# One-hot compares with a pointer scalar, and a second feature gathered in unit 0 (recommendation tower, one core)

## The reference, cut to what matters

```python
e = jnp.stack([tbl_0[ids[:, 0]], ..., tbl_26[ids[:, 26]]], axis=1)    # 2048 x 27 x 128
dot_products = jnp.einsum('bnd,bmd->bnm', e, e)
r, c = np.tril_indices(27, k=-1)
z = dot_products[:, c, r].reshape(2048, -1)
h = jnp.concatenate([z, dense_ctx], axis=1)                           # 2048 x 367
h = jnp.maximum(h @ W_top1 + b_top1, 0.0)                             # 512
h = jnp.maximum(h @ W_top2 + b_top2, 0.0)                             # 256
y = h @ W_top3
```

## Time and profile before

| what | us |
|---|---|
| median of three runs | 354.51 (354.46 to 360.79) |
| the profiled execution | 354.21 |
| its span, first to last instruction | 352.1 |
| around the span (354.21 - 352.1) | 2.1 |

### The profile page before, as it was taken

The page is one execution under the profiler, slowest core; times in us unless marked ns, Lnnn a source line. Parts: engine busy times, 40 slices in busy tenths (PEclk is TensorE's granted clock), DMA queues, the critical chain, the costliest instruction groups (busy, mean ns, idle before and its releaser), DMA issues.

```text
span 352.1 us, 12745 instructions
## 1 busy us (share of the span) xinstructions
PE 330.7 (94%) x5664; PEld 278.9 (79%) x5664; DVE 250.9 (71%) x335; ACT 148.8 (42%) x304; POOL 244.4 (69%) x265
## 2 busy tenths in 40 slices
PE   1897879999999999999999999999999999999986
PEld 0686768888888888888888888888888888887775
DVE  3899999989839696587929698487938786420322
ACT  2256543443534254433644245442545246535321
POOL 5777776777777777777777777777777777777100
PEclk9999999999999999999999999999999999999999
DMA  7997574443433433243332433243342332222000
GB/s 219 323 270 244 128 217 104 99 116 92 122 85 90 108 85 103 55 119 85 90 94 77 107 99 80 77 114 85 89 98 59 83 95 71 57 57 59 20 4 3
DMA packets 21928, 36.81 MB, mean 105 GB/s; under 512 B 7907, under 2 KB 12003, under 8 KB 21874
## 3 DMA queue, kind: packets, MB, share of 16 engines
q0 software_dynamic: 8256, 16.92, 19.7%
q1 hardware_dynamic: 13474, 18.55, 18.0%
q10 hardware_dynamic: 144, 0.52, 0.4%
HBM read 35.97 MB, written 0.01 MB: 102 GB/s over the span
## 4 chain that ended last, share of the span: by engine, by line
PE 87%; DVE 8%; issue 2%; DMA 1%; ACT 1%; SPq 0%; DVEq 0%
PE e_banks L560 42%; PE g_banks L594 13%; PE w_banks L624 10%; PE e_banks L572 9%; PE w_banks L655 8%; DVE one_hot L781 5%; DVE table_lo L762 3%; PE w_banks L644 2%; DMA ids_wide<-in_ids 1%; PE w_banks L613 1%; PE w_banks L666 0%; DVE g_banks L768 0%; DVE a L829 0%; ACT et L410 0%; DVE zt L795 0%
## 5 line engine op out<-in xcount | busy, mean ns | idle before, releaser
L528 POOL DMA_INDIRECT rows<-in_tbl,idx x258 | 243.6, 944 | 82.1 <-issue 77.4
L781 DVE TENSOR_TENSOR one_hot<-ids_wide,row_no 128x1024 fp32r<-128x1024 int32 x160 | 183.9, 1216 | 25.4 <-PE e_banks L560 21.4
L560 PE MATMUL e_banks<-one_hot,table_hi 128*128 128x512 f32 (+1 forms) x448 | 151.8, 356 | 5.3 <-issue 5.1
L560 PE MATMUL e_banks<-one_hot,table_lo 128*128 128x512 f32 (+1 forms) x448 | 147.2, 345 | 0.0
L560 PEld LDWEIGHTS e_banks<-one_hot,table_hi 128*128 128x128 f32 x448 | 85.5, 191 | 18.3 <-issue 7.6
L560 PEld LDWEIGHTS e_banks<-one_hot,table_lo 128*128 128x128 f32 x448 | 85.6, 191 | 9.2
L410 ACT ACTIVATE et<-e_banks 128x256 f32<-128x256 f32 x56 | 38.9, 694 | 84.7 <-PE e_banks L560 84.5
L402 ACT ACTIVATE et<-e_banks 128x512 f32<-128x512 f32 (+1 forms) x66 | 44.0, 668 | 51.5 <-PE e_banks L572 50.3
L795 DVE STREAM_TRANSPOSE zt<-g_banks 128x352 f32<-128x352 f32 (+1 forms) x32 | 17.8, 595 | 53.2 <-PE g_banks L594 53.2
L594 PEld LDWEIGHTS g_banks<-et 128*26 128x26 f32 x4096 | 42.0, 103 | 16.9 <-issue 13.2
L594 PE MATMUL g_banks<-et 128*26 128x26 f32 x4096 | 49.8, 191 | 1.2
(11 more groups left out here) (32 smaller groups left out, 111.1 us busy)
## 6 DMA issues: line engine op xcount, KB each, us to landing
ids_wide<-in_ids SPq DMA_DIRECT2D x31, 256.0 KB
et<-in_kept_tables SPq DMA_DIRECT2D x10, 512.0 KB, 9.9
rows<-in_tbl,idx POOLq DMA_INDIRECT x258
ids_wide<-in_ids SPq DMA_DIRECT2D x18, 128.0 KB
et<-in_kept_tables ACTq DMA_DIRECT2D x1, 512.0 KB, 3.9
a1T<-in_ids SPq DMA_DIRECT2D x4, 128.0 KB, 10.3
w<-in_w SPq DMA_DIRECT2D x2, 256.0 KB
w<-in_W_top SPq DMA_DIRECT2D x1, 512.0 KB
```

Source lines behind the costliest of these rows:

```text
L528: pool.indirect_dma_start(rows[:, k % RING, a, :], None, tables[f], bass.IndirectOffsetOnAxis(ap=idx[:, t, f:f + 1], axis=0)).then_inc(row ...
L560: last = nc.tensor.matmul(e_bank[n % E_BANKS][:, 0:UNIT * units_of((u, q))], part[:, q, c, :], hot_piece(o, piece)[:, i, :], start=(c == 0 ...
L781: nc.vector.tensor_tensor(hot_piece(o, piece), ids_place(o).unsqueeze(1).broadcast_to(shape), row_no[:, chunks[0]:chunks[-1] + 1].unsqueez ...
```

## The change

One feature more (q = 1, feature 4) is gathered for the two tiles of unit 0, so there are 260 gathers, nine look-ups in unit 0, and 172 pieces. `row_no` moves from PSUM to SBUF. A piece is no longer one `tensor_tensor` over 1024 numbers with both inputs broadcast, but one `tensor_scalar` for each row number, with that row number as a per-partition scalar: four of 256 numbers in a narrow piece, two of 512 in a wide one. PE's first look-ups of unit 1 wait for the table that they read, not for all eleven.

```diff
-GATHERED_IN = {0: 1}
+GATHERED_IN = {0: 2}
...
         row_no_i = sb("row_no_i", [P, OC], I32)
+        row_no = sb("row_no", [P, OC])
...
-        row_no = psum("row_no", [P, OC])
...
                 if u == 0:
                     pe.wait_ge(hi_ready, o + 1)
                     pe.wait_ge(lo_ready, o + 1)
-                elif o == FIRST_LOOK_UPS:
-                    pe.wait_ge(hi_ready, NOH)
-                    pe.wait_ge(lo_ready, NOH)
+                elif u == 1:
+
+                    pe.wait_ge(hi_ready, TABLE_ORDER.index(q) + 1)
+                    pe.wait_ge(lo_ready, TABLE_ORDER.index(q) + 1)
...
-                shape = [P, len(chunks), UNIT * units_of(LOOK_UPS[o])]
-                nc.vector.tensor_tensor(
-                    hot_piece(o, piece),
-                    ids_place(o).unsqueeze(1).broadcast_to(shape),
-                    row_no[:, chunks[0]:chunks[-1] + 1].unsqueeze(2).broadcast_to(shape),
-                    ALU.is_equal).then_inc(one_hot_ready, 1)
+                for i, c in enumerate(chunks):
+                    last = nc.vector.tensor_scalar(hot_piece(o, piece)[:, i, :], ids_place(o), row_no[:, c:c + 1], None,
+                                                   ALU.is_equal)
+                last.then_inc(one_hot_ready, 1)
```

## The result

The kernel after takes 375.61 us (median of 4 runs, 374.32 to 377.31), the kernel before in the same comparison 355.1; the ratio of the fast runs is 1.0566, 95% interval 1.0511 to 1.0622. The forecast was 363.6, slower by 2.6%. The direction held, and gathers are held up as forecast; the loss is more than twice the forecast one, and part of it comes by another way. The same kernel, run again in a later experiment, took 370.23 us, ratio 1.0477 (1.0413 to 1.054).

The account below looks back on a forecast made before the run. The prediction took DVE to pace unit 0, PE the rest, with POOL's gathers a hidden second bound. A 350.5 us span plus 11 for held gathers plus 2.1 around it made 363.6 us; range 352 to 388.

Parts of the forecast that it names:

- a second bound in POOL's "issue" time: POOL issues 258 gathers without pause, 0.30 us before nearly each; 77.4 of 82.1 us idle before gathers is issue.
- a gather waits for one compare: On POOL, a gather starting while a fast compare runs waits for that compare's end; 363.6 us, chance 0.45.
- Gathers aren't held: Rival: on POOL, waiting gathers slip in beside DVE's compares at no cost; 352.6 us, chance 0.16.
- gathers wait for whole pieces: Rival: DVE's back-to-back compares leave no gap, so gathers wait for a piece; 35 us delay, 387.6 us, chance 0.15.
- single rate: Rival: DVE's new compares run at the single rate and hold no gathers; 355.5 us, chance 0.15.
- Full exclusion: Rival: DVE's compares run only between POOL's gathers, adding 124 us; 477 us, chance 0.04.
- the delay: Time POOL's gathers are held by single compares over the run: 11 us, taken between 8.0 and 14.2, bounds 0 and 35.
- the rule: For POOL's gathers: delay is the sum of length squared / 2 over all compares, divided by the gathers' distance (1.29 us).
- 30.3 us of work that the change doesn't touch: The tail, from chunk 63's transpose on PE to the end of the span, taken over unchanged at 30.3 us.
- unit 0 ends 4 to 11 us earlier: Cheaper compares and fewer look-ups save DVE 11.3 us at most, so PE leaves unit 0 between 4 and 11 us earlier.
- forecast span 361.5: Whole kernel: 350.5 us if POOL keeps its pace, plus 11 for held gathers, makes 361.5 us of span.
- only 1.6 us of this gain: Of unit 0's 4 to 11 us, only 1.6 reach the end if POOL keeps its pace.

Follow-up runs that it names:

- the two partial kernels: The kernel after with fast compares in the narrow look-ups alone (358.72 us, ratio 1.0118) or in the wide look-ups alone (371.91 us, 1.0482), old compares elsewhere.

## Why the prediction was right or wrong

**Right: POOL takes over as the bound.** The forecast read a second bound in POOL's "issue" time. After the change the chain is POOL's for 60% (first profile), with 20% of "issue". With a quarter of the gathers it is PE's again and the loss is gone.

**Right: a gather waits for one compare, not for a piece and not for nothing.** The median gather isn't held (945 ns), 58 of the 62 that start within a compare of 512 are, and in two runs the longest is held 0.34 us. In the other runs with all gathers and fast compares one to four of 260 are held longer; the longest, beside the compares with a constant, takes 2.16 us. The sums by width are 2.2 and 16.0 us. "Gathers aren't held" and "gathers wait for whole pieces" (13 and 22 us in the two partial kernels) fall, and so does "single rate": a compare of 512 at that rate has a record of 680 ns, and the kernel after has 498. "Full exclusion" falls with compares that run beside gathers, as the one at 147.98 does.

**Mis-sized: the delay.** The term was 11 us; 13.8 and 14.7 were measured. It lies inside the bounds of the forecast, but 11 was only the middle between 8.0 and 14.2, and the prices behind it were too low: a pointer scalar makes a compare of 512 take 0.40 us, not 0.34. With a constant, where the prices are the forecast's, 11.9 us were measured. That the middle is so near is in part luck, since the rule counts the narrow compares, which hold almost nothing.

**Wrong: "30.3 us of work that the change doesn't touch".** This is the step that failed most. The work is the same, its time isn't: 38.0 us in the first profile, 33.0 in the repeat. The rows of the first profile give 7.6 of the 7.7 us. Behind its wait for chunk 63's rows PE is granted a lower clock (0.68 from 335 to 340 us): the 24 products cost 7.92 - 5.36 = 2.6 us more, the four transposes 0.4. PE then stands still twice for "issue", 1.14 and 0.93 us, and only behind these stops the clock falls again (0.50 from 365 to 370 us): the last layer costs 5.49 - 3.00 = 2.5 us more. Just before the stops PE ran at full clock (1.00 from 345 to 360 us), and the kernel with the old compares has the stops and a slow last layer (4.44) with no wait for rows at all. So some 3.0 us come through the held gathers, in this profile alone, and the rest, like most of the repeat's 2.7, comes with the nine look-ups in unit 0: the forecast counted what one look-up fewer saves PE and put its effect on the tail at nothing.

The DMA queues have packets ahead of both stops. In 355 to 364 us of the first profile there are two packets and no others, both of instructions:

```profile
q8 instruction: 2, 0.03, 1.6%
```

They start at 356.70 and 360.03, and the stops end 2.2 and 2.6 us behind, at 358.91 and 362.64; with the old compares it is 337.06 and 340.36, and 339.24 and 342.69. The stops lie 128 products apart, and a packet is 16384 bytes. The author's estimate from these figures is that PE waits for the next piece of its own program, and that fourteen products fewer, or 37 more, shift where in the work that falls. No run changes this alone, so it isn't shown.

**The sum put right.** Of the first profile, forecast span 361.5, measured 375.5: the first gather starts at 6.04 instead of 4.26, +1.8; held 13.8 instead of 11, +2.8; chunk 63 is turned 337.53 - 334.18 = 3.4 us behind the end of its last gather instead of 1.5, +1.9; the tail +7.7. That makes 14.2, where 14.0 are missing. Of the repeat, 367.7: start -0.3, held +3.7, chunk 63 +0.2, tail +2.7, together 6.3, where 6.2 are missing. The two ends of POOL's work in the first profile, its first gather and chunk 63's last:

```profile
6.04 1.10 POOL L528 DMA_INDIRECT rows<-in_tbl,idx  x1 [4.48 <-DMA idx<-in_idx]
...
333.23 0.95 POOL L528 DMA_INDIRECT rows<-in_tbl,idx  x1 [0.30 <-issue]
```

The late start is a late transfer of the indices (4.48 us of waiting, 2.71 before). For chunk 63's late rows the packets show a likely reason. Of the last gather's 65600 bytes 61500 came from 334.90 to 335.33; from 335.30 to 336.17 ran a packet of 16384 bytes of instructions; the last 4100 bytes came among the next gather's, up to 337.02.

**Price wrong, gain not settled, without weight: unit 0 ends 4 to 11 us earlier.** One narrow look-up with its table takes 3.48 us, not 2.81. The reasons are the price of the pointer scalar, 8 x 0.06 = 0.5 us for each look-up, and that DVE is held by gathers in turn: the compares of 256 have records of 382 ns in the mean where the median of those on `hT` is 341, and of 346 in the mean with a quarter of the gathers. With a constant a look-up with its table takes 2.75 us, as the forecast had it. Chunk 10, the first turned after unit 0, is turned by PE at 69.76 us in the first profile (where the gathers began 1.8 us later) and at 64.78 in the repeat. Before it was this row:

```profile
69.30 0.60 PE L572 MATMUL e_banks<-ident_r,rows 128*128 128x128 f32 x4
```

So the repeat won 4.5 us, just inside the forecast, and the first profile nothing. The kernel with idle products, the same up to there, turns the chunk at 68.03, the one with the old compares at 67.58. The spread between executions is as large as the gain, and some of it comes with one gathered feature more and not with the compares. It had no weight because POOL sets the end: the forecast let only 1.6 us of this gain through.

**Not told apart.** The kernel after took 375.61 us in the first comparison and 370.23 in the second, both against its own runs of before; the intervals of the two ratios overlap. The rows put the difference in the late start, chunk 63's landing and the tail. Whether the clock falls behind a wait isn't settled by the wait's length alone: one of 2.19 us was followed by slow transposes, one of 2.45 us (before the chunk at 330.90 of the same profile) by quick ones. What tips it wasn't tried.

## What to carry to other kernels

An engine with a low busy share can be a bound (POOL here, 69% busy): read its idle time by the reason, and where it is "issue" before every instruction, add instructions times (duration + gap) and compare with the span. Before making a DVE operation faster, or moving one of its inputs to SBUF, look at what POOL runs at that time: here gathers took 944 ns beside compares with an input in PSUM, 997 beside fast compares from SBUF and 1198 beside compares at the old rate with both inputs from SBUF. As an estimate from these runs, a faster form is paid with half its length squared, times its count, over the distance of POOL's instructions (for compares of 0.40 us 15.4 us where 16.0 were measured, for those of 0.26 us 5.1 where 2.2 were). And a tail isn't a constant (here 30.3 us before, 38.0 and 33.0 after): in one profile PE waited 2.96 us for rows ahead of it and stopped twice within it, and was granted 0.68 and 0.50 of its clock in two stretches behind that. So compare the tail with that of a run that has the new order of work and the old instructions.

## What the runs showed of the hardware that was not expected

- A compare of 1024 numbers at the slow rate (1.13 us from start to start) with both inputs in SBUF holds gathers for up to 1.05 us each, 65.6 us in all, and the kernel takes 18% longer; with one input in PSUM it holds none (944 ns in the mean).
- A scalar read per partition costs about 0.06 us per compare over a constant: compares of 256 numbers on `hT` have a median of 341 ns against 278.
- PE stops for 0.65 to 1.4 us, and each stop ends 2.2 to 2.9 us behind the start of a packet of instructions in a DMA queue; with 37 more products ahead of them, of the two stops one of 0.37 us was left.
- With few gathers a gather can wait far longer than one compare: the longest of the 66 beside fast compares took 4.48 us. With so many fewer of them it cost nothing there.
- PE's Gram products (4096, on a tile of the features) are quicker in the kernels with a quarter of the gathers, whose other rows are constants: this row is the one with the old compares. Each lasts 191 ns, as in the kernel before, but their busy time is 43.6 instead of 49.8 us, so they overlap more. These 6.2 us are most of the 7.4 by which that kernel's span (344.7) is shorter than before; the cause wasn't looked for.

```profile
L597 PE MATMUL g_banks<-et 128*26 128x26 f32 x4096 | 43.6, 191 | 0.3 <-issue 0.3
```
